# Read-out sums over four tokens with the products interleaved, and a second product buffer in the keys' place

## The chip, the cores and the metric

The kernel runs on one core of one Trainium2 chip. The metric is the device time of one execution in microseconds (us), lower is better. The engines are PE (TensorE; PEld is its weight load), DVE (VectorE), ACT (ScalarE), POOL (GpSimd) and SP, which only issues DMAs.

## What is computed

A vision tower: 32 images of 64 tokens with 256 features go through four layers, each with a mixer, a feed-forward part and layer norms. The change touches only the mixer of the second layer, a delta rule with 16 heads of 16 features (h = head, k, v = features):

```python
def step(S, inp):
    qt, kt, vt, at, bt = inp
    Sd = at[..., None, None] * S
    u = vt - jnp.einsum('bhk,bhkv->bhv', kt, Sd)
    Sn = Sd + bt[..., None, None] * kt[..., None] * u[:, :, None, :]
    o = jnp.einsum('bhk,bhkv->bhv', qt, Sn)
    return (Sn, o)
...
_, o = jax.lax.scan(step, S0, (tfirst(q), tfirst(k), tfirst(v), tfirst(a), tfirst(beta)))
o = o * jax.lax.rsqrt(jnp.mean(o * o, -1, keepdims=True) + EPS)
```

It is a recurrence over the 64 tokens. The read-out `o` of a token, the last line of the step, doesn't feed the next token.

## The kernel before

All data is fp32. In the delta layer (`delta_layer`) a partition holds one image and head for each of CG = 4 groups g, so that one state of a partition is 4 x 16 x 16 = 1024 numbers (g, v, k). It lies in two PSUM banks; the states of even and odd tokens have two banks each (`S[0]`, `S[1]`), and `halves` h = 0, 1 are the groups 0-1 and 2-3. Each engine runs its own program in order, and they meet at semaphores. One token t of the loop `for t in range(TOK)` is:

- DVE `read_keys(t)` (L1823, two halves of 512 elements): state times scaled key, PSUM to the tile `prod` (named made in the trace). It needs the state after token t-2; the effect of token t-1 is added as a column. Then DVE sums 18 numbers for each v (`tensor_reduce`, L1856) into `u`, which raises `u_made`.
- POOL makes the correction column of token t+1 (L1925), then the outer product `outer` of key and u (L1930, 1024 elements, tile xT_d in the trace).
- ACT places the values of a later token (L1603), writes the faded state of token t over the other pair of banks (`fade`, L1611, four instructions), and copies the fourth group's state to SBUF (`copy_last_group`, L1620), which raises `state_copied`.
- PE adds the outer product to the state in PSUM (`add_outer`, L1467): two matmuls of 512 columns with the identity as weights. An fp32 matmul shows as two records in the profile, so these are four records.
- Read-out of token j: DVE multiplies three groups of the state with the query (`read_queries(j)`, L1831, 768 elements, at its token j+3), POOL the fourth group (`read_copy(j)`, L1899, 256 elements, at its token j+2). The products go to the tile of the queries (chain_q), as `(r s n k)`: ring of two, two tokens s, 64 sums n = (g, v), and the 16 terms k next to each other. PE sums over k with the identity: `sum_pair(n, half)` (L1477) issues 8 matmuls of 128 columns (2 tokens x 64) behind `add_outer` of a token, 16 for a pair, so 16 records for each token. The moving operand takes one number in 16. ACT copies the 128 sums to the output tile (`store_pair`, L1624).
- Three times the squares of a stretch of outputs (CUTS) are made on ACT (`square_out`) and summed on PE (`sum_squares`, L1486), 32 records spread over six tokens.

PE's sums of token t stand between `add_outer(t)` and `add_outer(t+1)` in its queue. Pairs 0 to 30 (tokens 0 to 61) are read out that way; the last two tokens by DVE alone (`read_last`, L1839 and L1841). Behind the loop come the last squares, a Newton step and the norm of the outputs (L1871), which go out by DMA to the next stage.

The keys' tile (chain_k) is last read ahead of the loop, by `scale_keys` on DVE (L1796) and POOL (L1885).

Of the kernel before, what the change touches and what calls it, by code (L numbers as in the profile page):

```python
# [13 lines left out]
ALU = mybir.AluOpType  # L14
ACT = mybir.ActivationFunctionType
AX = mybir.AxisListType
# [10 lines left out]
TOK = 64  # L27
# [4 lines left out]
HD = D // HEADS  # L32
# [16 lines left out]
CG = 4  # L49
# [24 lines left out]
def bcast(ap, axis, n):  # L74

    ap = ap.unsqueeze(axis)
    shape = [int(s) for s in ap.shape]
    shape[axis] = n
    return ap.to_broadcast(shape)
# [1162 lines left out]


YS = 4
CUTS = (0, 18, 36, 52)
IN_STEPS = len(CUTS) - 1
TAIL = 2
LASTS = ((CUTS[-1], TOK - TAIL), (TOK - TAIL, TOK))
LAST = TOK - CUTS[-1]
ROW = HD + 2  # L1250
DIRECT = CG - 1
SUM_PARTS = ((0, 3), (3, 6), (6, 9), (9, 12), (12, 14), (14, HD))
# [29 lines left out]
def delta_layer(nc, sem, io, banks, H, ident, minus_half, token_rows, gate, chains, rates, front, chain, all_sent,  # L1282
# [15 lines left out]
    q, k, v, o = (chain[n] for n in "qkvo")  # L1298
    ka, kb, qt = (chain[n] for n in ("ka", "kb", "q_by_time"))
# [10 lines left out]
    prod = [prod_ring[:, i, :, :, :] for i in range(2)]  # L1310
    squares = w[:, :, :].rearrange("p c n -> p (c n)")[:, 0:HD * CG * CUTS[1]].rearrange("p (d n) -> p d n", d=HD)
    n_last = CG * HD * (TOK - TAIL - CUTS[-1])
    last_squares = [flat[:, n_prod + a:n_prod + b].rearrange("p (g d t) -> p g d t", g=CG, d=HD)
# [5 lines left out]
    Sc = [Sc_ring[:, i, :, :] for i in range(2)]  # L1319
    u_ring = rows_flat[:, n_zero + n_copy:n_zero + n_copy + 2 * CG * HD].rearrange("p (r g v) -> p r g v", r=2, g=CG)  # L1320
    u = [u_ring[:, i, :, :] for i in range(2)]
    products = q[:, :, :, :].rearrange("p g d t -> p (g d t)").rearrange("p (r s n k) -> p r s n k", r=2, s=2, k=HD)
    link = rate[:, :, 0, :]

    def state(b):
        return banks[:, b:b + 2, :].rearrange("p b (g v k) -> p (b g) v k", v=HD, k=HD)

    S = [state(0), state(2)]
    o_sum = [banks[:, b, 0:2 * CG * HD] for b in (5, 7)]
    halves = [slice(2 * h, 2 * h + 2) for h in range(2)]  # L1330
    summed_early, summed_late = slice(0, CUTS[-1]), slice(CUTS[-1], TOK)
    outs = [chains[n].rearrange("g (b h) (d t) -> g h d b t", h=HEADS, d=HD) for n in "qkv"]

    def o_n2(n):
        return banks[:, 6, CG * CUTS[n]:CG * CUTS[n + 1]].rearrange("p (g t) -> p g t", g=CG)

    def chunk_squares(n):
        return squares[:, :, 0:CG * (CUTS[n + 1] - CUTS[n])]
# [82 lines left out]
    def tensor(pe):  # L1421
# [41 lines left out]
        def add_outer(t, h):  # L1463
            if t:
                pe.wait_ge(sem(f"faded{h}"), t)
            pe.wait_ge(sem("outer_made"), t + 1)
            pe.matmul(S[t % 2][:, halves[h], :, :], ident[:, :], outer[t % 2][:, halves[h], :, :], start=False,  # L1467
                      stop=True, skip_group_check=True).then_inc(sem(f"state{h}"), 1)

        def sum_pair(n, half):  # L1470
            if half == 0:
                pe.wait_ge(sem("q_made"), 2 * n + 2)
                pe.wait_ge(sem("q_copy_made"), 2 * n + 2)
                if n > 1:
                    pe.wait_ge(sem("o_made"), n - 1)
            for k in range(HD // 2 * half, HD // 2 * (half + 1)):
                ins = pe.matmul(o_sum[n % 2].rearrange("p (s n) -> p s n", s=2), ident[:, :],  # L1477
                                products[:, n % 2, :, :, k], start=(k == 0), stop=(k == HD - 1))
            if half:
                ins.then_inc(sem("o_summed_pair"), 1)  # L1480

        def sum_squares(n, part):
            if part == 0:
                pe.wait_ge(sem("o_squared"), n + 1)
            for d in range(*SUM_PARTS[part]):
                ins = pe.matmul(o_n2(n), ident[:, :], chunk_squares(n)[:, d, :]  # L1486
                                .rearrange("p (g t) -> p g t", g=CG), start=(d == 0), stop=(d == HD - 1))
            if part == len(SUM_PARTS) - 1:
                ins.then_inc(sem("o_summed"), 1)
# [49 lines left out]
        for b in (1, 0):  # L1539
            for h in range(2):  # L1540
                ins = pe.matmul(banks[:, 2 * b + h, :], ident[:, :], zeros, start=True, stop=True)
                if b == 0:
                    ins.then_inc(sem(f"state{h}"), 1)
        for t in range(TOK):
            for h in range(2):
                add_outer(t, h)
            if t >= 3:
                sum_pair((t - 3) // 2, (t - 3) % 2)
            for n in range(IN_STEPS):
                if 0 <= t - CUTS[n + 1] - 5 < len(SUM_PARTS):  # L1550
                    sum_squares(n, t - CUTS[n + 1] - 5)
        sum_pair((TOK - TAIL) // 2 - 1, 1)

    def scalar(act):
        def norm(t):
# [46 lines left out]
        def place_values(t):  # L1602
            act.copy(prod[t % 2][:, :, :, HD + 1], v[:, :, :, t]).then_inc(sem("values_placed"), 1)  # L1603
# [12 lines left out]
        def copy_last_group(j):  # L1616
            act.wait_ge(sem("state1"), j + 2)
            if j >= 2:
                act.wait_ge(sem("q_copy_made"), j - 1)
            act.copy(Sc[j % 2], S[j % 2][:, DIRECT, :, :]).then_inc(sem("state_copied"), 1)  # L1620

        def store_pair(n):
            act.wait_ge(sem("o_summed_pair"), n + 1)
            act.copy(o[:, :, :, 2 * n:2 * n + 2], o_sum[n % 2].rearrange("p (s g d) -> p g d s", s=2, g=CG)  # L1624
                     ).then_inc(sem("o_made"), 1)

        def mean_out(n):
# [7 lines left out]
            act.activation(rn[:, :, at], rn[:, :, at], ACT.Exp, scale=-0.5).then_inc(sem("on_guess"), 1)  # L1635

        def square_out(n):
            act.wait_ge(sem("o_made"), CUTS[n + 1] // 2)
            if n:
                act.wait_ge(sem("o_summed"), n)  # L1640
            act.square(chunk_squares(n).rearrange("p d (g t) -> p g d t", g=CG),
                       o[:, :, :, CUTS[n]:CUTS[n + 1]]).then_inc(sem("o_squared"), 1)
# [69 lines left out]
        for t in range(TOK):  # L1712
            if t + 2 < TOK:
                act.wait_ge(sem("u_made"), t + 1)
                place_values(t + 2)
            if t:
                fade(t, 0)
                fade(t, 1)
            if 0 < t < TOK - 1:
                copy_last_group(t - 1)  # L1720
            if t >= 5 and t % 2:
                store_pair((t - 5) // 2)
            for n in range(IN_STEPS):
                if t == CUTS[n + 1] + 4:
                    square_out(n)
                if t == CUTS[n + 1] + 5 + len(SUM_PARTS):
                    mean_out(n)
        store_pair((TOK - TAIL) // 2 - 1)
        act.wait_ge(sem("on_mean"), IN_STEPS)
        guess(summed_early, 1)  # L1730
        act.wait_ge(sem("o_made"), (TOK - TAIL) // 2)
        square_last(0)
        act.wait_ge(sem("last_o"), 2)
        square_last(1)
# [4 lines left out]
    def vector(dve):  # L1739
        once = Tally(dve, sem("dve_once"))  # L1740
# [83 lines left out]
                                  bcast(ka[:, t, halves[h], :], 2, HD), ALU.mult).then_inc(sem(f"prod_made{h}"), 1)  # L1824

        def read_queries(j):
            n = j // 2
            dve.wait_ge(sem("state_copied"), j + 1)
            if n >= 2:
                dve.wait_ge(sem("o_summed_pair"), n - 1)  # L1830
            dve.tensor_tensor(products[:, n % 2, j % 2, 0:DIRECT * HD, :].rearrange("p (g v) k -> p g v k", g=DIRECT),  # L1831
                              S[j % 2][:, 0:DIRECT, :, :], bcast(qt[:, j, 0:DIRECT, :], 2, HD), ALU.mult
                              ).then_inc(sem("q_made"), 1)

        def read_last(j):
            for h in range(2):
                dve.wait_ge(sem(f"state{h}"), j + 2)
                dve.wait_ge(sem(f"faded{h}"), TOK - 1)
            once.mark(dve.tensor_tensor(prod[j % 2][:, :, :, 0:HD], S[j % 2], bcast(qt[:, j, :, :], 2, HD), ALU.mult))  # L1839
            once.settle()  # L1840
            dve.tensor_reduce(o[:, :, :, j], prod[j % 2][:, :, :, 0:HD], AX.X, ALU.add).then_inc(sem("last_o"), 1)  # L1841

        for t in range(TOK):
            if t == 3:
# [10 lines left out]
                dve.wait_ge(sem("outer_made"), t - 1)  # L1855
            dve.tensor_reduce(u[t % 2], prod[t % 2], AX.X, ALU.add).then_inc(sem("u_made"), 1)  # L1856
        read_queries(TOK - 3)
        dve.wait_ge(sem("u_made"), TOK)
        read_last(TOK - 2)
        read_last(TOK - 1)  # L1860
        for n, (a, b) in enumerate(LASTS):
            dve.wait_ge(sem("last_squared"), n + 1)
            once.mark(dve.tensor_reduce(n2[:, :, a:b], last_squares[n].rearrange("p g d t -> p g t d"), AX.X, ALU.add))
# [10 lines left out]
    def gpsimd(pool):  # L1874
# [17 lines left out]
            pool.tensor_tensor(dots, k[:, g, :, 1:], k[:, g, :, 0:TOK - 1], ALU.mult).then_inc(sem("neighbours"), 1)  # L1892

        def read_copy(j):
            n = j // 2
            pool.wait_ge(sem("state_copied"), j + 1)
            if n >= 2:
                pool.wait_ge(sem("o_summed_pair"), n - 1)
            pool.tensor_tensor(products[:, n % 2, j % 2, DIRECT * HD:CG * HD, :], Sc[j % 2],  # L1899
                               bcast(qt[:, j, DIRECT, :], 1, HD), ALU.mult).then_inc(sem("q_copy_made"), 1)  # L1900

        for t in range(T):
# [33 lines left out]
        x, y, z = (b[:, :, summed_early] for b in (n2, rn, tmp))  # L1936
# [1060 lines left out]
```

## Time and profile before

| | |
|---|---|
| median of 3 runs | 1424.85 us (1424.39 to 1436.09) |
| profiled execution: its own time | 1427.18 us |
| profiled execution: span from first to last instruction | 1425.2 us |
| mean granted TensorE clock | 0.953 of 2.4 GHz |
| busy in the span | PE 89%, DVE 55%, ACT 37%, POOL 33% |
| the delta layer's token loop | from 655.6 us, first DVE product, to 1009.5 us, start of the output norm |

The profile comes from one execution, so that durations and starts are of that one. Times in its views are from the start of the span. A group of the views is named by source line, engine and operation, then output and inputs; a busy time of overlapping instructions counts once.

### The profile page before, as it was taken

How to read it: one execution, taken by the hardware profiler on the slowest of the kernel's cores; microseconds unless marked ns; L12 is line 12 of the kernel's file. 1: busy time of each engine (PE TensorE's matmuls, PEld its weight loads, DVE VectorE, ACT ScalarE, POOL GpSimd, SP SyncE). 2: the span in 40 equal slices, each digit the busy share in tenths (PEclk: the TensorE clock that was granted, in tenths of full speed). 3: DMA queues.
4: the chain of work that ended last, by engine and by line, in shares of the span. 5: the costliest groups of instructions: out<-in, count | busy, mean ns of one | idle time of the engine just before them, and what ended most of it. 6: DMA issues, size and time to landing. Idle time of an engine off the chain costs nothing. (4 is left out here: it accounts for less than half of the span.)

```text
span 1425.2 us, 25953 instructions
## 1 busy us (share of the span) xinstructions
PE 1268.6 (89%) x9667; PEld 1022.5 (72%) x9667; DVE 788.2 (55%) x1721; ACT 531.5 (37%) x1318; POOL 464.6 (33%) x635
## 2 busy tenths in 40 slices
PE   7999994999999999873999999999589999978975
PEld 5666673888999999621777778777477777756753
DVE  4666666111121221798666666665467777642587
ACT  3554541121112121544444444343134444434456
POOL 0111111232333331544555455554122121101465
PEclk9999996999999999996999999999799999999985
DMA  4111102998888883790000000000200004006721
GB/s 144 31 46 46 35 13 74 354 369 316 323 316 335 316 324 133 194 267 2 1 1 1 0 1 0 1 1 1 78 12 11 11 9 182 2 1 253 220 73 60
DMA packets 82717, 162.31 MB, mean 114 GB/s; under 512 B 42977, under 2 KB 61537, under 8 KB 76577
## 3 DMA queue, kind: packets, MB, share of 16 engines
q1 hardware_dynamic: 63776, 114.44, 23.6%
q0 software_dynamic: 10224, 44.05, 8.0%
q10 hardware_dynamic: 8592, 2.16, 0.7%
q8 instruction: 78, 1.28, 0.4%
q14 instruction: 47, 0.38, 0.1%
HBM read 134.28 MB, written 26.35 MB: 113 GB/s over the span
## 5 line engine op out<-in xcount | busy, mean ns | idle before, releaser
L1477 PEld LDWEIGHTS banks<-chain_q,ident 128*128 128x128 f32 x992 | 202.8, 204 | 39.3 <-issue 24.2
L1477 PE MATMUL banks<-chain_q,ident 128*128 128x128 f32 x992 | 226.2, 394 | 0.0
L936 PE MATMUL banks<-rowsT,w_up 128*128 128x128 f32 x1716 | 201.2, 278 | 0.3 <-DMA w_up<-in_up_w 0.3
L936 PEld LDWEIGHTS banks<-rowsT,w_up 128*128 128x128 f32 x1716 | 198.0, 195 | 0.6 <-DMA w_up<-in_up_w 0.5
L1467 PE MATMUL banks<-xT_d,ident 128*128 128x512 f32 x256 | 124.4, 607 | 32.0 <-POOL xT_d L1930 28.1
L1611 ACT ACTIVATE banks<-banks,rate 128x256 f32<-128x256 f32 x252 | 100.6, 445 | 131.5 <-DVE made L1823 128.6
L1930 POOL TENSOR_TENSOR xT_d<-kb,ys 128x1024 f32<-128x1024 f32 x64 | 123.3, 1927 | 3.1 <-DVE ys L1856 3.0
L1823 DVE TENSOR_TENSOR made<-banks,ka 128x512 f32<-128x512 f32 x128 | 87.8, 690 | 58.2 <-PE banks L1467 52.7
L950 PE MATMUL banks<-w_down,hT 128*128 128x256 f32 x468 | 107.5, 379 | 0.6 <-DVE res L1115 0.6
L1105 DVE TENSOR_TENSOR hT<-banks,silu 64x128 f32<-64x128 f32 x39 | 11.0, 282 | 166.7 <-ACT silu L993 166.7
L1467 PEld LDWEIGHTS banks<-xT_d,ident 128*128 128x128 f32 x256 | 48.5, 197 | 68.7 <-issue 29.9
L950 PEld LDWEIGHTS banks<-w_down,hT 128*128 128x128 f32 x468 | 85.9, 190 | 11.0 <-issue 1.0
L1856 DVE TENSOR_REDUCE ys<-made 128x64 f32<-128x1152 f32 x64 | 86.6, 1353 | 5.7
L878 POOL DMA_DIRECT2D w_down<-in_down_w x39 | 22.2, 569 | 188.6 <-PE banks L950 180.4
L1831 DVE TENSOR_TENSOR chain_q<-banks,q_by_time 128x768 f32<-128x768 f32 x62 | 59.1, 953 | 41.2 <-PE banks L1477 41.2
L2090 POOL TENSOR_TENSOR agg_b<-agg_b,minus_half 128x1 f32<-128x1 f32 x48 | 28.4, 591 | 161.2 <-DVE agg_b L2316 160.0
L1925 POOL TENSOR_TENSOR made<-ys,rate 128x64 f32<-128x64 f32 x63 | 19.6, 311 | 155.5 <-DVE ys L1856 155.5
L983 ACT COPY rowsT<-banks 128x256 f32<-128x256 f32 x39 | 14.5, 373 | 145.6 <-PE banks L114 145.6
L468 PE MATMUL banks<-w_tok,patches 128*128 128x256 f32 x192 | 52.2, 411 | 6.7 <-DMA patches<-in_patches 6.7
L1115 DVE COPY res<-banks 128x256 f32<-128x256 f32 x39 | 16.6, 425 | 75.2 <-PE banks L950 75.2
L108 PE MATMUL banks<-ident 128*128 128x128 f32 x328 | 43.8, 291 | 12.1 <-PEq L92 12.1
L108 PEld LDWEIGHTS banks<-ident 128*128 128x128 f32 x328 | 41.9, 205 | 13.5 <-issue 13.0
(330 smaller groups left out, 2381.7 us busy)
## 6 DMA issues: line engine op xcount, KB each, us to landing
w_up<-in_up_w SPq DMA_DIRECT2D x39, 1408.0 KB, 5.9
w_down<-in_down_w POOLq DMA_DIRECT2D x39, 768.0 KB, 4.9
inter<-res_x SPq DMA_DIRECT2D x16, 512.0 KB, 2.8
back<-inter SPq DMA_DIRECT2D x15, 512.0 KB, 3.9
patches<-in_patches SPq DMA_DIRECT2D x16, 384.0 KB, 3.3
f<-in_f SPq DMA_DIRECT2D x6, 1024.0 KB, 11.7
ys<-token_rows SPq DMA_DIRECT2D x16, 256.0 KB, 2.9
xn_rows<-xn_all SPq DMA_DIRECT2D x16, 128.0 KB, 1.7
```

The costliest lines, as they stand in the source:

```text
L108: pe.matmul(out, ident, ident, start=True, stop=True, skip_group_check=True)
L468: ins = pe.matmul(X, patches[t % SLOTS_IN][:, c, :], w_tok[:, c, :], start=(c == 0), stop=(c == PC - 1), skip_group_check=True)
L936: ins = pe.matmul(out[:, m * P:(m + 1) * P], w[:, c, m * P:(m + 1) * P], x[:, c, :], start=(c == 0), stop=(c == 1))
L950: ins = pe.matmul(Y, hT[j % 2][:, c, :], w_down[j % DEEP][:, c, :], start=(c == 0), stop=(c == FULL))
L1467: pe.matmul(S[t % 2][:, halves[h], :, :], ident[:, :], outer[t % 2][:, halves[h], :, :], start=False, stop=True, skip_group_check=True).th ...
L1477: ins = pe.matmul(o_sum[n % 2].rearrange("p (s n) -> p s n", s=2), ident[:, :], products[:, n % 2, :, :, k], start=(k == 0), stop=(k == HD ...
L1611: ins = act.activation(S[t % 2][:, g, :, :].rearrange("p v k -> p (v k)"), S[(t + 1) % 2][:, g, :, :].rearrange("p v k -> p (v k)"), ACT.Copy,
L1823: dve.tensor_tensor(prod[t % 2][:, halves[h], :, 0:HD], S[t % 2][:, halves[h], :, :], bcast(ka[:, t, halves[h], :], 2, HD), ALU.mult).then ...
L1831: dve.tensor_tensor(products[:, n % 2, j % 2, 0:DIRECT * HD, :].rearrange("p (g v) k -> p g v k", g=DIRECT), S[j % 2][:, 0:DIRECT, :, :], ...
L1856: dve.tensor_reduce(u[t % 2], prod[t % 2], AX.X, ALU.add).then_inc(sem("u_made"), 1)
L1930: pool.tensor_tensor(outer[t % 2], bcast(kb[:, t, :, :], 2, HD), bcast(u[t % 2], 3, HD), ALU.mult).then_inc(sem("outer_made"), 1)
L2090: pool.tensor_tensor(agg[n][:, 1:2], agg[n][:, 1:2], minus_half[:, 0:1], ALU.pow).then_inc(sem(f"ln{n}_rstd"), 1)
```

## The change

- `sum_quad(m, part)` takes the place of `sum_pair`: four tokens (QUAD) are summed at once. A part is 4 matmuls of 256 columns, one part behind `add_outer` of each token from t = 5 on; so a token has 8 records of 256 columns in the place of 16 of 128.
- The products of four tokens are interleaved: `(n k s)`, so that the four tokens of one product stand next to each other and the terms k are four numbers apart. DVE and POOL write one number in four; PE reads runs of four numbers, 64 numbers apart.
- The ring of two buffers is now one in the queries' tile and one in the keys' tile (each whole).
- ACT's `store_quad` copies 256 sums for four tokens once, at every fourth token.
- TAIL is 4: quads 0 to 14 (tokens 0 to 59) are summed on PE. The products of tokens 60 and 61 are made as before, and summed by DVE (`sum_last(0, 2)`, 2048 terms); those of 62 and 63 are made by `read_last` into the same interleaved buffer and summed by `sum_last(2, 4)`.
- The first cut moves from 18 to 20, the squares' sums and means by a token, and the last `mean_out` behind the loop.

```diff
-CUTS = (0, 18, 36, 52)
+CUTS = (0, 20, 36, 52)
...
-TAIL = 2
+QUAD = 4
+TAIL = QUAD
+QUADS = (TOK - TAIL) // QUAD
...
-    products = q[:, :, :, :].rearrange("p g d t -> p (g d t)").rearrange("p (r s n k) -> p r s n k", r=2, s=2, k=HD)
+    products = [x[:, :, :, :].rearrange("p g d t -> p (g d t)").rearrange("p (n k s) -> p n k s", k=HD, s=QUAD)
+                for x in (q, k)]
...
     def state(b):
...
-    o_sum = [banks[:, b, 0:2 * CG * HD] for b in (5, 7)]
+    o_sum = [banks[:, b, 0:QUAD * CG * HD] for b in (5, 7)]
...
-        def sum_pair(n, half):
-            if half == 0:
-                pe.wait_ge(sem("q_made"), 2 * n + 2)
-                pe.wait_ge(sem("q_copy_made"), 2 * n + 2)
-                if n > 1:
-                    pe.wait_ge(sem("o_made"), n - 1)
-            for k in range(HD // 2 * half, HD // 2 * (half + 1)):
-                ins = pe.matmul(o_sum[n % 2].rearrange("p (s n) -> p s n", s=2), ident[:, :],
-                                products[:, n % 2, :, :, k], start=(k == 0), stop=(k == HD - 1))
-            if half:
-                ins.then_inc(sem("o_summed_pair"), 1)
+        def sum_quad(m, part):
+            if part == 0:
+                pe.wait_ge(sem("q_made"), QUAD * (m + 1))
+                pe.wait_ge(sem("q_copy_made"), QUAD * (m + 1))
+                if m > 1:
+                    pe.wait_ge(sem("o_made"), m - 1)
+            for k in range(HD // QUAD * part, HD // QUAD * (part + 1)):
+                ins = pe.matmul(o_sum[m % 2].rearrange("p (n s) -> p n s", s=QUAD), ident[:, :],
+                                products[m % 2][:, :, k, :], start=(k == 0), stop=(k == HD - 1))
+            if part == QUAD - 1:
+                ins.then_inc(sem("o_summed_quad"), 1)
         def sum_squares(n, part):
...
-            if t >= 3:
-                sum_pair((t - 3) // 2, (t - 3) % 2)
+            if t >= QUAD + 1:
+                sum_quad((t - QUAD - 1) // QUAD, (t - QUAD - 1) % QUAD)
...
-                if 0 <= t - CUTS[n + 1] - 5 < len(SUM_PARTS):
-                    sum_squares(n, t - CUTS[n + 1] - 5)
-        sum_pair((TOK - TAIL) // 2 - 1, 1)
+                if 0 <= t - CUTS[n + 1] - 6 < len(SUM_PARTS):
+                    sum_squares(n, t - CUTS[n + 1] - 6)
+        sum_quad(QUADS - 1, QUAD - 1)
     def scalar(act):
         def norm(t):
...
-        def store_pair(n):
-            act.wait_ge(sem("o_summed_pair"), n + 1)
-            act.copy(o[:, :, :, 2 * n:2 * n + 2], o_sum[n % 2].rearrange("p (s g d) -> p g d s", s=2, g=CG)
+        def store_quad(m):
+            act.wait_ge(sem("o_summed_quad"), m + 1)
+            act.copy(o[:, :, :, QUAD * m:QUAD * (m + 1)], o_sum[m % 2].rearrange("p (g d s) -> p g d s", s=QUAD, g=CG)
...
         def mean_out(n):
...
         def square_out(n):
-            act.wait_ge(sem("o_made"), CUTS[n + 1] // 2)
+            act.wait_ge(sem("o_made"), CUTS[n + 1] // QUAD)
...
-            if t >= 5 and t % 2:
-                store_pair((t - 5) // 2)
+            if t > 2 * QUAD and t % QUAD == 1:
+                store_quad((t - 2 * QUAD - 1) // QUAD)
...
-                if t == CUTS[n + 1] + 4:
+                if t == CUTS[n + 1] + 5:
...
-                if t == CUTS[n + 1] + 5 + len(SUM_PARTS):
+                if t == CUTS[n + 1] + 6 + len(SUM_PARTS):
...
-        store_pair((TOK - TAIL) // 2 - 1)
+        store_quad(QUADS - 1)
+        mean_out(IN_STEPS - 1)
...
-        act.wait_ge(sem("o_made"), (TOK - TAIL) // 2)
+        act.wait_ge(sem("o_made"), QUADS)
...
         def read_queries(j):
-            n = j // 2
+            m = j // QUAD
...
-            if n >= 2:
-                dve.wait_ge(sem("o_summed_pair"), n - 1)
-            dve.tensor_tensor(products[:, n % 2, j % 2, 0:DIRECT * HD, :].rearrange("p (g v) k -> p g v k", g=DIRECT),
+            if m >= 2:
+                dve.wait_ge(sem("o_summed_quad"), m - 1)
+            dve.tensor_tensor(products[m % 2][:, 0:DIRECT * HD, :, j % QUAD].rearrange("p (g v) k -> p g v k", g=DIRECT),
...
-            once.mark(dve.tensor_tensor(prod[j % 2][:, :, :, 0:HD], S[j % 2], bcast(qt[:, j, :, :], 2, HD), ALU.mult))
-            once.settle()
-            dve.tensor_reduce(o[:, :, :, j], prod[j % 2][:, :, :, 0:HD], AX.X, ALU.add).then_inc(sem("last_o"), 1)
+            once.mark(dve.tensor_tensor(products[QUADS % 2][:, :, :, j % QUAD].rearrange("p (g v) k -> p g v k", g=CG),
+                                        S[j % 2], bcast(qt[:, j, :, :], 2, HD), ALU.mult))
+        def sum_last(a, b):
+            dve.tensor_reduce(o[:, :, :, TOK - QUAD + a:TOK - QUAD + b].rearrange("p g d s -> p (g d) s"),
+                              products[QUADS % 2][:, :, :, a:b].rearrange("p n k s -> p n s k"), AX.X, ALU.add
+                              ).then_inc(sem("last_o"), 1)
...
-        dve.wait_ge(sem("u_made"), TOK)
+        dve.wait_ge(sem("q_made"), TOK - 2)
+        dve.wait_ge(sem("q_copy_made"), TOK - 2)
+        sum_last(0, 2)
...
+        once.settle()
+        sum_last(2, QUAD)
...
         def read_copy(j):
-            n = j // 2
+            m = j // QUAD
...
-            if n >= 2:
-                pool.wait_ge(sem("o_summed_pair"), n - 1)
-            pool.tensor_tensor(products[:, n % 2, j % 2, DIRECT * HD:CG * HD, :], Sc[j % 2],
+            if m >= 2:
+                pool.wait_ge(sem("o_summed_quad"), m - 1)
+            pool.tensor_tensor(products[m % 2][:, DIRECT * HD:CG * HD, :, j % QUAD], Sc[j % 2],
```

## Rows read from the trace of the kernel before

**Rows 1.** The page: busy time of each engine.

```profile
PE 1268.6 (89%) x9667; PEld 1022.5 (72%) x9667; DVE 788.2 (55%) x1721; ACT 531.5 (37%) x1318; POOL 464.6 (33%) x635
```

**Rows 2.** Stretches of the token loop: us, then busy us of each engine, granted clock.

```profile
660.75:672.60 11.85, 8.02 (x12) 2.44 (x12) 8.71 (x12) 5.55 (x16) 7.37 (x8) 0.84 0.00 0
680.00:780.00 100.00, 100.00 (x387) 78.15 (x386) 69.41 (x78) 45.82 (x129) 54.71 (x58) 1.00 0.00 1
```

**Rows 3.** Groups of the loop, 655 to 1010 us: busy us, mean ns | idle before.

```profile
L1477 PE MATMUL banks<-chain_q,ident 128*128 128x128 f32 x992 | 226.2, 394 | 0.0
...
L1856 DVE TENSOR_REDUCE ys<-made 128x64 f32<-128x1152 f32 x64 | 86.6, 1353 | 5.7
L1831 DVE TENSOR_TENSOR chain_q<-banks,q_by_time 128x768 f32<-128x768 f32 x62 | 59.1, 953 | 41.2 <-PE banks L1477 41.2
...
L1899 POOL TENSOR_TENSOR chain_q<-ys,q_by_time 128x256 f32<-128x256 f32 x62 | 45.2, 729 | 0.0
...
L1925 POOL TENSOR_TENSOR made<-ys,rate 128x64 f32<-128x64 f32 x63 | 19.6, 311 | 155.5 <-DVE ys L1856 155.5
...
L1486 PE MATMUL banks<-w_delta,ident 128*128 128x72 f32 x64 | 8.7, 268 | 0.0
```

**Rows 4.** Order of time, tokens 3 and 4, without sums: start, us.

```profile
668.85 1.35 DVE L1856 TENSOR_REDUCE ys<-made 128x64 f32<-128x1152 f32 x1
...
670.12 0.96 DVE L1831 TENSOR_TENSOR chain_q<-banks,q_by_time 128x768 f32<-128x768 f32 x1
...
670.54 1.93 POOL L1930 TENSOR_TENSOR xT_d<-kb,ys 128x1024 f32<-128x1024 f32 x1
671.00 1.28 DVE L1823 TENSOR_TENSOR made<-banks,ka 128x512 f32<-128x512 f32 x2
671.76 1.54 ACT L1611 ACTIVATE banks<-banks,rate 128x256 f32<-128x256 f32 x4 [1.21 <-DVE made L1823]
672.37 1.35 DVE L1856 TENSOR_REDUCE ys<-made 128x64 f32<-128x1152 f32 x1
...
672.63 1.98 PE L1467 MATMUL banks<-xT_d,ident 128*128 128x512 f32 x4 [1.53 <-ACT banks L1611]
673.21 0.40 ACT L1620 COPY ys<-banks 128x256 f32<-128x256 f32 x1
```

**Rows 5.** Order of time, one token in the middle.

```profile
816.65 0.42 PEld L1467 LDWEIGHTS banks<-xT_d,ident 128*128 128x128 f32 x2
...
818.60 3.65 PE L1477 MATMUL banks<-chain_q,ident 128*128 128x128 f32 x16
...
821.86 0.21 PEld L1467 LDWEIGHTS banks<-xT_d,ident 128*128 128x128 f32 x1
```

**Rows 6.** Order of time, matmuls of 256 columns in another stage.

```profile
303.31 2.76 PE L950 MATMUL banks<-w_down,hT 128*128 128x256 f32 x12
```

**Rows 7.** Groups around the loop: accesses with a step, and one held op.

```profile
L1788 DVE SCALAR_TENSOR_TENSOR f<-rn,rate 128x64 f32<-128x64 f32 x4 | 9.5, 2383 | 0.1
...
L1796 DVE TENSOR_TENSOR ka<-chain_k,f 128x1024 f32<-128x1024 f32 x4 | 7.7, 1922 | 0.1
...
L1871 DVE TENSOR_TENSOR chain_o<-chain_o,rn 128x1024 f32<-128x1024 f32 x4 | 4.6, 1221 | 0.0
...
L1863 DVE TENSOR_REDUCE n<-made 128x40 f32<-128x640 f32 x1 | 1.3, 1281 | 5.9 <-ACT made L1646 5.9
...
L1863 DVE TENSOR_REDUCE n<-made 128x8 f32<-128x128 f32 x1 | 0.3, 282 | 0.0
...
L1885 POOL TENSOR_TENSOR kb<-chain_k,f 128x1024 f32<-128x1024 f32 x4 | 9.4, 2360 | 13.0 <-DVE f L1784 13.0
```

**Rows 8.** Order of time, end of the loop.

```profile
987.24 1.35 DVE L1856 TENSOR_REDUCE ys<-made 128x64 f32<-128x1152 f32 x1
...
997.57 7.14 PE L1477 MATMUL banks<-chain_q,ident 128*128 128x128 f32 x32
...
1009.53 4.63 DVE L1871 TENSOR_TENSOR chain_o<-chain_o,rn 128x1024 f32<-128x1024 f32 x4
```


## Prediction

> **What bounds the kernel now.** I read the page first: PE is busy for 89% of the span, far ahead of the others [rows 1], but that is an average over four layers. The change touches only the token loop, so I cut out that stretch. Between 680 and 780 us PE is busy for 100.00 of 100 us at full granted clock, DVE for 69, POOL for 55 and ACT for 46 [rows 2]. PE is the bound there, and the groups of the loop say with what: 992 records of the read-out sums hold 226.2 us [rows 3].
>
> The order of time gives the token's sum. One token in the middle takes 821.86 - 816.65 = 5.21 us [rows 5]. Its 16 sum records take 3.65 us; the last has a tail of 0.39 (mean of one [rows 3]), so that they follow each other every (3.65 - 0.39)/15 = 0.217 us, 3.47 us a token. What is left for the four records of the outer product is 5.21 - 3.47 = 1.74 us. Squares come on top: 8.7 us / 64 = 0.136 us a record [rows 3], 96 records, 13 us in the whole loop.
>
> What else could be the bound is shown by the trace too. In tokens 3 and 4 the read-out products are already made, but no sums are queued yet: there DVE's reductions start at 668.85 and 672.37, 3.52 us apart [rows 4]. Between them DVE has no gap: reduction, query products (670.12), key products (671.00), next reduction. So 3.52 us is DVE's own token, 1.7 us below PE's. POOL needs 0.31 + 1.93 + 0.73, about 3.0 us [rows 3, 4]; ACT's fades and state copy are 1.54 + 0.40 [rows 4] and its copy of 64 values is small, about 2.3 us. Both fit.
>
> **PE's part of the change.** Removed: 16 records of 128 columns a token. Added: 8 records of 256. The trace doesn't show a moving operand in runs of four, so I bound it. From below: contiguous matmuls of 256 columns, 12 in 2.76 us with a tail of 0.38, are (2.76 - 0.38)/11 = 0.216 us each [rows 6]. From above: the columns cost what they cost now, 2 x 0.217 = 0.434 us. Today's 0.217 for 128 columns is as much as 256 contiguous ones take, so today's step of 64 bytes doubles the time of a column. The new operand has that kind of step once in four numbers. I take the lower end, 0.216, because three of four numbers are read as the contiguous rows' are; halfway cases are checked below. PE's token is then 1.74 + 8 x 0.216 = 3.47 us, and 3.47 + 0.82 = 4.29 us in the twelve tokens that also carry six records of squares.
>
> The Trainium skill (SBUF — State Buffer, the note on cachelines in its section on the DMA port swizzle) says that SBUF is read in lines of 16 bytes and that accesses to the same line run at full bandwidth, with two hits enough. By it the new reads, four numbers of one line, would cost the contiguous price, as in my sum; today's doubled column agrees with it.
>
> **DVE's part.** `read_queries` keeps its 768 elements and 953 ns [rows 3], but now writes one number in four. No row has a write with a step of 16 bytes. Lower end: nothing extra; a reduction over data with a step of 8 bytes takes 282 ns for 128 elements [rows 7], which is the same 155 ns + 1.04 ns an element that contiguous work has (1353 ns for 1152 [rows 3]). Upper end: a DVE product that writes with a step of 256 bytes takes 1922 ns for 1024 elements, its contiguous sister 1221 [rows 7]; a reduction that reads with a step of 40 bytes takes 1281 ns for 640 [rows 7]. Both are 155 ns + 1.73 to 1.76 ns an element. At that price the query products take 155 + 768 x 1.73 = 1480 ns, 0.53 us more. Between the ends I take the upper one: the row at 256 bytes is the only one of the same operation with the step on its output, and the penalty has its full size at 40 bytes already, so it looks like one that is paid or not, with nothing between. DVE's token becomes 3.52 + 0.53 = 4.05 us.
>
> **POOL and ACT.** `read_copy` writes with the same step. Its row is 729 ns [rows 3]; the POOL product with a strided output takes 2360 ns against 1927 without [rows 4, 7], 0.42 ns an element, so 256 elements cost 0.11 us at most. POOL's token is 3.1 us of 4.05: covered, also without the cover of DVE's price, as 3.1 is under 3.52. ACT's copy of 256 sums comes once in four tokens, about 0.4 us, and the first squares grow from 18 to 20 tokens; ACT has 2.3 us of work plus these in 4.05. In the three tokens where copy and squares (1.3 us) meet it is about 4.0 us: just covered, and a slip there costs some tenths.
>
> **Waits.** PE's part 0 of a quad waits for DVE's product of the fourth token and POOL's of the same token, and `add_outer` of the next token queues behind it. In the time of tokens 3 and 4, the matching product of DVE begins at 670.12 and would end at 671.60, POOL's begins when its outer product ends (672.47) and ends by 673.3; PE's four outer records run from 672.63 to about 674.35. So both are there before PE asks [rows 4]. In the other direction DVE and POOL wait for a free buffer at every fourth token, for sums that PE ends at about 672.63 + 3.47 = 676.1; DVE asks one token and more later (672.37 + 4.05 + 1.35 = 677.8). Nothing new stalls. PE's longer tokens with squares exceed 4.05 by 0.24 for four tokens in a row, about 1 us; the state's first half is summed by 672.63 + 0.87 = 673.5, and DVE takes it at 671.00 + 3.52 = 674.5 in the present rhythm [rows 4] and 0.5 us later in the new one, some 1.5 us of slack, so this is hidden.
>
> **The loop.** Before: from the reduction of token 3 at 668.85 to that of token 63 at 987.24 [rows 4, 8] are 318.4 us for 60 tokens. After: 60 x 4.05 = 243.0, and 0.5 for the products made before, 243.5 us. Gain 74.9 us.
>
> **The tail.** Before, from the last reduction's start to the output norm: 1009.53 - 987.24 = 22.3 us, held by PE, which is three tokens late and ends its sums at 997.57 + 7.14 = 1004.7 [rows 8]. After, PE's backlog is gone: outer product of token 63 about 3.4 us behind the reduction's start, end of the sums at about 8.7. DVE now has the longer chain. It can sum tokens 60 and 61 when POOL's last copy is made, at 1.35 + 0.1 + 1.93 + 0.84 = 4.2; that is 2048 terms with a step of 16 bytes, 155 + 2048 x 1.73 = 3.70, to 7.9; two products of 1024 at 1.93, to 11.8; the second sum 3.70, to 15.5. From the last output to the norm there were 1009.53 - 1004.7 = 4.8 us before [rows 8]; the early guess and most squares now lie beside DVE's sums, so I take 3.5, and come to 19.0. Gain 3.3 us. At contiguous prices the same chain is 4.2 + 2.28 + 2 x 1.22 + 2.28 + 3.3 = 14.5, a gain of 7.8.
>
> **Sum.** 74.9 + 3.3 = 78 us from the profiled execution's 1427.2 us gives 1349; the median of the runs is 2.3 below that execution, so 1346 us. The work behind the loop starts from its output and moves with it: the DMAs there are issued at the end of the loop.
>
> **Rivals.**
>
> *DVE's step is free.* For it: the reduction with a step of 8 bytes. Then DVE's token is 3.52 and PE's 3.47 plus squares. DVE gives 211 us for 60 tokens; of the 13 us of squares some 9 don't fit beside it: 220, a gain of 98, and the tail's 7.8: 106 us, 1319 us. Against it: only reads at 8 bytes support it. The same note of the Trainium skill says both that an access which changes the line pays and that a stride of 4 fp32 is free; by its first sentence the forecast holds, by its second this rival, at 1319 us.
>
> *PE gains nothing.* If 256 columns in runs of four still take 0.434, PE's token is 1.74 + 3.47 = 5.21 as before, and DVE's dearer products hide under it. Only the tail moves, by some 3 us of DVE that lie beside PE's backlog: 1420 to 1425 us. It decides from 0.29 a record on, where 1.74 + 8 x 0.29 passes 4.05; at 0.33, halfway, the token is 4.36 plus squares, 4.55 on average, and the time about 1378. For it: today's strided columns cost double, and every new run starts a new line. Against it: the share of such numbers falls from all to a quarter.
>
> *Slower: DVE held by POOL.* A DVE operation of 64 elements took 2383 ns where POOL's product of 2360 ran [rows 7]; at 155 ns + 1.04 ns an element it would be 222. If the query products with their spread output were held so behind POOL's outer product, which starts 0.4 us after them [rows 4], DVE's token would be 4.05 + 1.93 = 5.98: 359 us for 60 tokens, 40 more than before, and 1465 us. It decides from a token of 5.3 us, 1.8 us of added product time. Against it: the held operation has both inputs in SBUF; the query products have one in PSUM, as now, and aren't held today.
>
> **How the numbers follow.** The forecast has a chance of 0.56, the free step 0.22, a PE record in between (1360 to 1400 us) 0.08, PE without gain 0.11, the held DVE 0.03. The range takes in the forecast, the free step with a margin for its tail, and most of the middle: 1312 to 1385 us, about 0.85. Within 1% (1411 to 1439, what this measurement can't tell from no change) lies PE without gain. Faster by over 1%: 0.86; same 0.11; slower 0.03.
>
> **What the changed profile would show.** Right: 480 records of 256 columns, spaced 0.22 us; query products of about 1480 ns; reductions 4.05 us apart, with DVE busy nearly without gaps and PE idle 0.4 to 0.6 us a token; the wait of DVE's key products for PE gone. Products of 950 ns would show the free step, with PE and DVE both near full at 3.6 us a token. Records 0.43 us apart would show PE without gain, products of 3 us the held DVE. The forecast is wrong most easily in the price of one number in four on DVE.

## The result and the profile after

The changed kernel takes 1352.87 us in the median of 4 runs (1350.19 to 1357.56), beside 1427.19 us for the kernel before in 4 runs (1424.39 to 1436.09). The ratio is 0.9473 with a 95% interval of [0.9421, 0.9525]. By the medians that is 74 us less. The forecast was 1346 us with a range of 1312 to 1385. Times of the experiments below are medians too; one execution of terms_outermost, longer than its others at a lower granted clock (1360.49 us), is counted neither in its median nor in its ratio.

The page of the changed kernel, span and busy times, beside [rows 1]:

```profile
span 1352.3 us, 24890 instructions
...
PE 1173.6 (87%) x9155; PEld 908.6 (67%) x9155; DVE 818.0 (60%) x1721; ACT 526.1 (39%) x1302; POOL 466.7 (35%) x635
```

PE gave up 95 us of work and 512 records; DVE took on 30 us. As shares of the span, 89 to 87% and 55 to 60%, both look small, since the span covers four layers. The stretch view of the token loop shows more, beside [rows 2]:

```profile
680.00:780.00 100.00, 91.50 (x301) 55.44 (x301) 97.63 (x100) 54.31 (x152) 71.07 (x74) 0.98 0.00 1
780.00:910.00 130.00, 123.17 (x451) 78.77 (x450) 127.13 (x129) 72.96 (x205) 92.48 (x98) 1.00 0.00 1
```

DVE, the third busy time behind the length, went from 69% to 98%, PE from 100% to 92 and 95%. The bound has moved. The groups of the loop, the view of [rows 3], say what each operation costs now:

```profile
L1864 DVE TENSOR_REDUCE ys<-made 128x64 f32<-128x1152 f32 x64 | 86.6, 1353 | 5.7
L1827 DVE TENSOR_TENSOR made<-banks,ka 128x512 f32<-128x512 f32 x128 | 82.1, 681 | 3.2 <-PE banks L1470 3.2
L1480 PE MATMUL banks<-chain_q,ident 128*128 128x256 f32 x256 | 61.8, 385 | 0.0
L1480 PE MATMUL banks<-chain_k,ident 128*128 128x256 f32 x224 | 52.9, 379 | 0.0
L1835 DVE TENSOR_TENSOR chain_q<-banks,q_by_time 128x768 f32<-128x768 f32 x32 | 50.3, 1571 | 0.0
...
L1835 DVE TENSOR_TENSOR chain_k<-banks,q_by_time 128x768 f32<-128x768 f32 x30 | 47.1, 1569 | 0.2 <-ACT ys L1623 0.2
...
L1911 POOL TENSOR_TENSOR chain_q<-ys,q_by_time 128x256 f32<-128x256 f32 x32 | 23.5, 735 | 0.0
```

The sums are 480 records with 114.7 us of busy time, half of 226.2 [rows 3]. DVE's query products cost 1570 ns instead of 953. POOL's fourth group costs 735 instead of 729. The idle time of DVE ahead of its query products, 41.2 us before, is gone.

One token without squares, in order of time, beside [rows 5]:

```profile
796.89 1.35 DVE L1864 TENSOR_REDUCE ys<-made 128x64 f32<-128x1152 f32 x1
...
798.17 1.57 DVE L1835 TENSOR_TENSOR chain_q<-banks,q_by_time 128x768 f32<-128x768 f32 x1
...
798.98 1.89 PE L1480 MATMUL banks<-chain_k,ident 128*128 128x256 f32 x8
...
799.57 1.28 DVE L1827 TENSOR_TENSOR made<-banks,ka 128x512 f32<-128x512 f32 x2
...
800.34 1.54 ACT L1614 ACTIVATE banks<-banks,rate 128x256 f32<-128x256 f32 x4 [1.73 <-DVE made L1827]
...
800.94 1.35 DVE L1864 TENSOR_REDUCE ys<-made 128x64 f32<-128x1152 f32 x1
...
801.21 1.98 PE L1470 MATMUL banks<-xT_d,ident 128*128 128x512 f32 x4 [0.34 <-ACT banks L1614]
```

The reductions are 800.94 - 796.89 = 4.05 us apart and DVE goes from one operation to the next. The eight sum records follow each other every (1.89 - 0.38)/7 = 0.216 us. PE stands idle for 0.34 us ahead of the outer product and waits for ACT's fade, which waits for DVE's key products.

The end of the loop, beside [rows 8]:

```profile
914.39 1.35 DVE L1864 TENSOR_REDUCE ys<-made 128x64 f32<-128x1152 f32 x1
...
918.54 3.83 DVE L1847 TENSOR_REDUCE chain_o<-chain_k 128x128 f32<-128x2048 f32 x1 [1.31 <-POOL chain_k L1911]
...
922.28 3.83 DVE L1843 TENSOR_TENSOR chain_k<-banks,q_by_time 128x1024 f32<-128x1024 f32 x2
...
922.74 1.95 PE L1480 MATMUL banks<-chain_q,ident 128*128 128x256 f32 x8
924.72 0.37 ACT L1627 COPY chain_o<-banks 128x256 f32<-128x256 f32 x1 [5.83 <-PE banks L1480]
...
926.14 3.77 DVE L1847 TENSOR_REDUCE chain_o<-chain_k 128x128 f32<-128x2048 f32 x1
```

PE's sums end at 924.7, DVE's at 929.9: the tail is now DVE's. The output norm starts at 932.93. The two profiled executions can be cut at the same four events, the starts of the first key product, of the reductions of tokens 3 and 63, and of the norm:

| stretch (us) | before | after | difference |
|---|---|---|---|
| start to first key product | 655.6 | 656.8 | +1.2 |
| to the reduction of token 3 | 13.2 | 13.7 | +0.5 |
| 60 tokens | 318.4 | 243.9 | -74.5 |
| tail, to the output norm | 22.3 | 18.5 | -3.8 |
| norm to end | 415.7 | 419.4 | +3.7 |
| span | 1425.2 | 1352.3 | -72.9 |

### The profile page after: what moved, and what is told of

It reads as the page before. It is cut to its first block and busy times, and to the rows that moved or that the text cites. A ratio compares the mean times of both kernels' runs of the same rounds, so it can differ in the third digit from the quotient of the medians.

```text
span 1352.3 us, 24890 instructions
## 1 busy us (share of the span) xinstructions
PE 1173.6 (87%) x9155; PEld 908.6 (67%) x9155; DVE 818.0 (60%) x1721; ACT 526.1 (39%) x1302; POOL 466.7 (35%) x635
## 5 line engine op out<-in xcount | busy, mean ns | idle before, releaser
L1470 PE MATMUL banks<-xT_d,ident 128*128 128x512 f32 x256 | 130.8, 635 | 46.5 <-POOL xT_d L1942 26.1
L1614 ACT ACTIVATE banks<-banks,rate 128x256 f32<-128x256 f32 x252 | 97.4, 448 | 108.9 <-DVE made L1827 107.0
L1470 PEld LDWEIGHTS banks<-xT_d,ident 128*128 128x128 f32 x256 | 44.4, 193 | 101.3 <-ACT banks L1614 66.7
L1827 DVE TENSOR_TENSOR made<-banks,ka 128x512 f32<-128x512 f32 x128 | 82.1, 681 | 3.2 <-PE banks L1470 3.2
L983 ACT COPY rowsT<-banks 128x256 f32<-128x256 f32 x39 | 14.5, 373 | 146.2 <-PE banks L114 146.2
L1480 PEld LDWEIGHTS banks<-chain_q,ident 128*128 128x128 f32 x256 | 49.6, 194 | 20.4 <-issue 15.1
L1480 PE MATMUL banks<-chain_q,ident 128*128 128x256 f32 x256 | 61.8, 385 | 0.0
L108 PE MATMUL banks<-ident 128*128 128x128 f32 x328 | 41.6, 282 | 15.5 <-PEq L92 15.5
L1480 PEld LDWEIGHTS banks<-chain_k,ident 128*128 128x128 f32 x224 | 42.6, 190 | 17.7 <-issue 13.4
L1480 PE MATMUL banks<-chain_k,ident 128*128 128x256 f32 x224 | 52.9, 379 | 0.0
L108 PEld LDWEIGHTS banks<-ident 128*128 128x128 f32 x328 | 39.9, 197 | 16.9 <-issue 16.4
```

Of the source, the lines that this page charges most:

```text
L108: pe.matmul(out, ident, ident, start=True, stop=True, skip_group_check=True)
L1480: ins = pe.matmul(o_sum[m % 2].rearrange("p (n s) -> p n s", s=QUAD), ident[:, :], products[m % 2][:, :, k, :], start=(k == 0), stop=(k == ...
L1614: ins = act.activation(S[t % 2][:, g, :, :].rearrange("p v k -> p (v k)"), S[(t + 1) % 2][:, g, :, :].rearrange("p v k -> p (v k)"), ACT.Copy,
L1827: dve.tensor_tensor(prod[t % 2][:, halves[h], :, 0:HD], S[t % 2][:, halves[h], :, :], bcast(ka[:, t, halves[h], :], 2, HD), ALU.mult).then ...
```

## The experiments

Each kernel was timed beside the kernel before, and its ratio is to that. The theory was the prediction's: PE's price is that of its read pattern, DVE's that of its write pattern, and the loop goes at the pace of the slower of the two. The rivals were that the number of instructions matters, that a chain of waits through PE and ACT sets the token, and that steps or runs have other prices than I took.

**wide_only.** Quads and 256 columns stay, the interleaving goes:

```diff
-    products = [x[:, :, :, :].rearrange("p g d t -> p (g d t)").rearrange("p (n k s) -> p n k s", k=HD, s=QUAD)
+    products = [x[:, :, :, :].rearrange("p g d t -> p (g d t)").rearrange("p (s n k) -> p n k s", k=HD, s=QUAD)
```

The order of tokens and sums in the PSUM bank is turned with it, and so is ACT's copy from there.

> Quads, 256 columns and the second buffer as in the change, but the products of a token lie contiguous again, (s n k), so that PE reads one number in sixteen. Theory (what halves PE's time is the run of four, not the width of the matmul): a record costs 2 x 0.217 = 0.434 us, PE's token 1.74 + 8 x 0.434 = 5.21 us plus squares, the query product is back at 0.95 us, and the time is 1420 to 1428 us, within 0.5% of the kernel before. Rival (the gain comes from half as many instructions): records of about 0.22 to 0.3 us and 1320 to 1375 us.

Measured: 1423.12 us in the median of 10 runs, ratio 0.9963 [0.9935, 0.9991]. A token in its order of time:

```profile
756.45 1.90 PE L1470 MATMUL banks<-xT_d,ident 128*128 128x512 f32 x4
758.18 3.61 PE L1480 MATMUL banks<-chain_k,ident 128*128 128x256 f32 x8
761.62 1.90 PE L1470 MATMUL banks<-xT_d,ident 128*128 128x512 f32 x4
```

Eight records take as long as sixteen did: (3.61 - 0.61)/7 = 0.429 us each, and 761.62 - 756.45 = 5.17 us a token. Half the instructions at twice the columns, together with the second buffer and the new tail, are worth 0.4%. The rival falls.

**plain_writes.** The changed kernel, with DVE and POOL writing to a contiguous view of the same buffers, PE reading as in the change:

```diff
+    plain = [x[:, :, :, :].rearrange("p g d t -> p (g d t)").rearrange("p (s n k) -> p n k s", k=HD, s=QUAD)
+             for x in (q, k)]
...
-            dve.tensor_tensor(products[m % 2][:, 0:DIRECT * HD, :, j % QUAD].rearrange("p (g v) k -> p g v k", g=DIRECT),
+            dve.tensor_tensor(plain[m % 2][:, 0:DIRECT * HD, :, j % QUAD].rearrange("p (g v) k -> p g v k", g=DIRECT),
...
-            pool.tensor_tensor(products[m % 2][:, DIRECT * HD:CG * HD, :, j % QUAD], Sc[j % 2],
+            pool.tensor_tensor(plain[m % 2][:, DIRECT * HD:CG * HD, :, j % QUAD], Sc[j % 2],
```

> The changed kernel, but DVE and POOL write each token's products contiguously (another place of the same buffer), while PE reads runs of four as in the change; so the outputs of tokens 0 to 61 are sums of other products. Only the price of the writes is taken away. Theory (DVE's 1.57 us product is the bound of the loop): product 0.95 us, token 3.52 to 3.65 us, 25 to 32 us below the changed kernel: 1322 to 1330 us. Rival (the token is set by the chain through PE and ACT, and DVE only looks full): less than 8 us gained, 1345 to 1352 us.

Measured: 1323.0 us (4 runs), ratio 0.9256 [0.9211, 0.9302]. Its products, and two reductions in order of time:

```profile
L1837 DVE TENSOR_TENSOR chain_q<-banks,q_by_time 128x768 f32<-128x768 f32 x32 | 30.6, 955 | 0.0
...
L1837 DVE TENSOR_TENSOR chain_k<-banks,q_by_time 128x768 f32<-128x768 f32 x30 | 28.6, 954 | 0.2 <-ACT ys L1625 0.2
...
796.95 1.35 DVE L1866 TENSOR_REDUCE ys<-made 128x64 f32<-128x1152 f32 x1
...
800.46 1.35 DVE L1866 TENSOR_REDUCE ys<-made 128x64 f32<-128x1152 f32 x1
```

The products are back at 955 and 954 ns. A token without squares takes 800.46 - 796.95 = 3.51 us, DVE's own token of before; those with squares take 3.9 to 4.1, and the 60 tokens 217.8 us, 3.63 on average. So the write pattern costs the changed kernel 26 us in the loop. No chain of waits held the token at 4.06.

Both engines' writes were changed here. That the price is DVE's own, and not a disturbance by POOL's writes (whose operation changed by 7 to 9 ns), is seen in the tail of the changed kernel, where POOL is done when DVE makes the last two products:

```profile
L1843 DVE TENSOR_TENSOR chain_k<-banks,q_by_time 128x1024 f32<-128x1024 f32 x2 | 3.8, 2001 | 0.0
```

(2001 - 155)/1024 = 1.80 ns a number, against (1570 - 155)/768 = 1.84 in the loop. The tail kept its step in plain_writes and its length of 18.5 us.

**half_sums.** Half of PE's sums left out:

```diff
-            for k in range(HD // QUAD * part, HD // QUAD * (part + 1)):
+            for k in range(HD // QUAD * part, HD // QUAD * (part + 1), 2):
...
-                                products[m % 2][:, :, k, :], start=(k == 0), stop=(k == HD - 1))
+                                products[m % 2][:, :, k, :], start=(k == 0), stop=(k == HD - 2))
```

> The changed kernel with every second term k left out of the sums on PE (2 matmuls a part instead of 4), so the read-outs of tokens 0 to 59 hold half their terms. PE's token falls by 0.87 us. Theory (PE has slack now): the loop keeps its 4.06 us and the time stays within 3 us of the changed kernel, 1348 to 1355 us. Rival (PE's sums still delay the next outer product): up to 0.3 us a token, 1330 to 1342 us.

Measured: 1348.95 us (4 runs), ratio 0.945 [0.9409, 0.9491], not told apart from the change. In order of time:

```profile
794.96 1.03 PE L1480 MATMUL banks<-chain_q,ident 128*128 128x256 f32 x4
...
797.19 1.98 PE L1470 MATMUL banks<-xT_d,ident 128*128 128x512 f32 x4 [1.20 <-ACT banks L1614]
```

The sums of a token take 1.03 us instead of 1.89, and PE's idle time ahead of the outer product grows by the same 0.86, from 0.34 to 1.20. The 60 tokens take 243.76 us against 243.85. With plain_writes this settles the bound from both sides: taking work from PE gives nothing; taking 0.6 us from DVE's product gives 0.54 us in a token without squares and 0.43 on average, because PE's squares then show.

**pairs_in_quad.** Two tokens interleaved instead of four:

```diff
-    products = [x[:, :, :, :].rearrange("p g d t -> p (g d t)").rearrange("p (n k s) -> p n k s", k=HD, s=QUAD)
+    products = [x[:, :, :, :].rearrange("p g d t -> p (g d t)").rearrange("p (w n k s) -> p w n k s", w=2, k=HD, s=2)
...
-                                products[m % 2][:, :, k, :], start=(k == 0), stop=(k == HD - 1))
+                                products[m % 2][:, :, :, k, :], start=(k == 0), stop=(k == HD - 1))
```

The writes of DVE and POOL, the place of the sums in PSUM and the copies follow it.

> As the change, but two tokens interleaved instead of four, (w n k s) with w = 2 pairs and s = 2: DVE and POOL write one number in two (8 bytes apart), PE reads 256 columns in runs of two. Theory (DVE's price is that of steps over 8 bytes, and two numbers side by side are enough for PE): products 0.95 us, records 0.22 us, DVE's token 3.52 and PE's 3.47 plus squares, so about 3.65 us a token instead of 4.06: 60 x 0.41 = 25 us below the changed kernel, and some 4 more at the tail, 1322 to 1330 us. Rival A (any step costs DVE the same): 1.5 us products, time as the changed kernel, 1350. Rival B (runs of two save PE only half): records of 0.33 us, PE's token 4.4, and 1370 to 1380 us.

Measured: 1321.62 us (5 runs), ratio 0.9254 [0.9214, 0.9295]. In order of time:

```profile
784.33 1.35 DVE L1865 TENSOR_REDUCE ys<-made 128x64 f32<-128x1152 f32 x1
...
785.60 0.95 DVE L1836 TENSOR_TENSOR chain_q<-banks,q_by_time 128x768 f32<-128x768 f32 x1
...
786.47 1.28 DVE L1828 TENSOR_TENSOR made<-banks,ka 128x512 f32<-128x512 f32 x2
...
786.82 1.92 PE L1480 MATMUL banks<-chain_k,ident 128*128 128x256 f32 x8
...
787.84 1.35 DVE L1865 TENSOR_REDUCE ys<-made 128x64 f32<-128x1152 f32 x1
```

The token is 3.51 us, DVE's old floor. A write with a step of 8 bytes costs DVE nothing (0.95 us), and PE reads runs of two at the rate of contiguous numbers, (1.92 - 0.38)/7 = 0.220 us for 256. The 60 tokens take 218.3 us and the tail 16.4; the tail's gain of 2.1 us is half of the 4 expected. Both rivals of this run fall.

The two sentences of the Trainium skill's note on cachelines (SBUF — State Buffer, section on the DMA port swizzle), which spoke for different outcomes, can be weighed now. Two numbers in a 16-byte line were enough for both engines (DVE 0.95 us, PE 0.220 a record), as its first sentence says, and one in a line paid (1.57 and 0.429). "4 fp32" was not a free stride for DVE's writes. Steps between 8 and 16 bytes weren't tried.

**pair_runs_only.** The kernel before, with its pairs interleaved and nothing else: no quads, no second buffer, no other tail:

```diff
-    products = q[:, :, :, :].rearrange("p g d t -> p (g d t)").rearrange("p (r s n k) -> p r s n k", r=2, s=2, k=HD)
+    products = q[:, :, :, :].rearrange("p g d t -> p (g d t)").rearrange("p (r n k s) -> p r n k s", r=2, s=2, k=HD)
...
-                                products[:, n % 2, :, :, k], start=(k == 0), stop=(k == HD - 1))
+                                products[:, n % 2, :, k, :], start=(k == 0), stop=(k == HD - 1))
```

The writes, the order in PSUM and ACT's copy follow it.

> The kernel before with one edit: the two products of a pair interleaved, (r n k s) with s = 2, in the same ring in the queries' tile. Still 16 records of 128 columns a token, no second buffer, no quads. Theory (runs of two numbers are what PE needs, and steps of 8 bytes cost DVE nothing): a record falls from 0.217 us to 0.11 to 0.12, PE's token to 1.74 + 16 x 0.115 = 3.6 us plus squares, products stay at 0.95 us; loop 3.65 to 3.8 us a token, 1320 to 1335 us. Rival (128 columns are too short beside their weight load of 0.19 us): records stay near 0.19 us, PE's token 4.8 us plus squares, 1395 to 1405 us.

Measured: 1321.66 us (4 runs), ratio 0.9234 [0.9187, 0.928]. A token:

```profile
783.82 1.95 PE L1477 MATMUL banks<-chain_q,ident 128*128 128x128 f32 x16
...
784.82 1.35 DVE L1856 TENSOR_REDUCE ys<-made 128x64 f32<-128x1152 f32 x1
...
788.33 1.35 DVE L1856 TENSOR_REDUCE ys<-made 128x64 f32<-128x1152 f32 x1
```

The records follow each other every (1.95 - 0.27)/15 = 0.112 us instead of 0.217, and a token takes 3.51 us; the 60 tokens 220.3, against 218.3 with quads. So the width of the matmul and the second buffer bring 2 us in the loop between them, which the medians don't tell apart. The rival, that the weight load holds a short matmul, falls: each load is still 0.188 us long while the records follow each other every 0.112, so the loads overlap. This small edit is faster than both kernels. It leads the changed one by 31 us, of which the traces show 23.6 in the loop and 3.0 in the tail.

**terms_outermost.** The 16 terms outermost, so that PE reads 256 contiguous numbers and DVE writes with a step of 1024 bytes:

```diff
-    products = [x[:, :, :, :].rearrange("p g d t -> p (g d t)").rearrange("p (n k s) -> p n k s", k=HD, s=QUAD)
+    products = [x[:, :, :, :].rearrange("p g d t -> p (g d t)").rearrange("p (k n s) -> p n k s", k=HD, s=QUAD)
```

> The changed kernel with the products as (k n s): the 256 numbers of one term lie together, so PE reads 256 contiguous numbers, and DVE and POOL write with a step of 1024 bytes instead of 16. Theory (DVE's price is paid for any step over a line, whatever its size, and PE's run of four already has the full rate): products 1.57 us as with 16 bytes, records 0.216 us, time as the changed kernel within 3 us, 1347 to 1356 us. Rival (the price grows with the step, or several numbers in one place collide): products of 2 us or more, and 1375 us or more.

Measured: 1342.89 us (3 runs, 1339.22 to 1349.69), ratio 0.9403 [0.9333, 0.9472]. Its products:

```profile
L1835 DVE TENSOR_TENSOR chain_q<-banks,q_by_time 128x768 f32<-128x768 f32 x32 | 49.0, 1531 | 0.0
```

The products take 1531 ns, hardly less than with 16 bytes, and PE's records are no faster than with runs of four (61.3 us of busy time for 256, against 61.8). Of the steps measured here, 8 bytes cost DVE nothing, and from 16 to 1024 bytes the price doesn't grow. The median is 4 us below the 1347 to 1356 us that I gave, so that number was missed. The mechanism was not: 60 tokens take 241.7 us, 2.2 less than in the change, by the 0.04 us of the product. The rest of its lead of 10 us lies behind the loop (last section), where the change did nothing.

**changed_again.** The changed kernel, to see how much of the table above is its own.

> The changed kernel once more, for its spread and a second trace of the stages behind the loop, which took 419.4 us in its first trace against 415.7 us in that of the kernel before. Theory (that difference is of the execution, not of the change): median 1350 to 1354 us, loop 243.9 us again to 0.3 us, and stages behind the loop that take another time than 419.4. Rival (a later stage is slower by the change): 419 to 420 us there again.

Measured: 1353.3 us (4 runs), ratio 0.9462 [0.941, 0.9513]. The loop takes 244.2 us again, the tail 18.5, and the stages from norm to end 416.3 instead of 419.4, beside 415.7 in the kernel before. The rival, that the change slows a later stage, finds no support.

## Why the prediction was right

By its own steps:

- *PE's part.* Forecast 0.216 us a record, measured 0.216. PE's own token of 3.47 us can't be read in the changed kernel, where PE waits 0.34 us in a token without squares (0.4 to 0.6 were forecast). That the width brings nothing and the run all of it is shown by wide_only (0.429) and pair_runs_only.
- *DVE's part.* The choice between no price and 1480 ns was the one that decided between 1346 and 1319. No row lay between 8 and 40 bytes, so it was a judgement. Measured 1570 ns, the upper end and 90 ns over. The reason given, that the penalty doesn't grow with the step, holds from 16 to 1024 bytes (1570 and 1531 ns). That the token is 4.05 us to the hundredth is luck: the product is 0.62 us longer, not 0.53, but the next operation starts 1.40 us behind its start, where it was 0.88 before (671.00 - 670.12 [rows 4]). So two operations overlap by 0.09 us more than before, which nobody forecast and no run explains, and 0.52 is left.
- *The free step as rival.* Its price was about right: 1319 forecast, with 220 us in the loop, and plain_writes has 1323 with 217.8. That kernel frees the step in the loop alone; its tail is 18.5 us, not the 14.5 of this rival. The rival was wrong for the change, since a step of 8 bytes is free and one of 16 is not. The row at 8 bytes tells the price of a step of 8 bytes, for a write too, as pairs_in_quad shows, and says nothing of 16.
- *POOL.* Forecast up to 0.11 us more, measured 0.006. Steps of 16 and of 1024 bytes both left it at 735 and 734 ns. The comparison was of two different operations, and it isn't shown what made the one in [rows 7] longer. POOL lay beside DVE's token either way.
- *Waits.* No wait of PE for products shows up in the waits. From the reduction of token 3 on, DVE waits in the loop twice: 0.3 us for PE's outer product and 0.2 for ACT's state copy. In the whole loop its key products wait 3.2 us for PE, against 52.7 before. The longer tokens with squares are hidden: the reductions stay 4.05 us apart there, and half_sums shortens PE's work in all and gains nothing.
- *The loop.* 243.5 forecast, 243.9 measured; gain 74.9 against 74.5. Sixty tokens of 4.05 are 243.0. Of the rest, 0.8 lies in three early tokens. PE had waited up to 2.3 us ahead of an outer product there, its granted clock was 0.67 and 0.61 in two stretches of 4 us, and in the second its eight records took 3.11 us instead of 1.89. The forecast had 0.5 us there, for another reason.

```profile
684.00:688.00 4.00, 4.00 (x9) 2.40 (x8) 3.70 (x5) 2.01 (x7) 2.88 (x3) 0.61 0.00 0
...
685.87 3.11 PE L1480 MATMUL banks<-chain_q,ident 128*128 128x256 f32 x8
```

- *The tail.* 19.0 against 18.5, with DVE as its bound; the two sums over 2048 numbers take 3.8 us each and were forecast at 3.7. DVE's last sum ends 15.5 us behind the last reduction's start, as forecast.
- *The held DVE, PE without gain and the record in between.* No product of 3 us; records at the lower end. All three fell, with 3%, 11% and 8%.

The 7 us between 1346 and 1352.9 are not in the loop or its tail, where the difference is 78.3 us (74.5 + 3.8), and 78.2 were forecast. In the profiled execution 1.2 us lie ahead of the loop and 3.7 behind it. The rest is that of the medians: the forecast took off the 2.3 us by which the profiled execution lay above the kernel before's median of three runs, and with a fourth run that distance is gone (1427.18 and 1427.19); the changed kernel's is 1.1 us (1353.92 and 1352.87). The sum itself, 1349 less 2.3, is 1346.7 and was written down as 1346.

## What to carry to other kernels

When one engine is full, ask of its instructions what rate they run at before asking for fewer of them: 128 columns in the time of 256 pointed to the read pattern, and a new order of the data gave nearly all of the gain (wide_only has the rest of the change and 0.4%). Look for the smallest such change: a pair side by side was enough for the reader and free for the writer, while four side by side moved the price to the writer, which then became the bound. The edit that only pairs the numbers gained 106 us where the larger change gained 74. And where a trace has a few rounds without the work of the busy engine, as tokens 3 and 4 here, read the next bound from them.

## What was not expected

The stages behind the loop are untouched, but took from 409.8 to 424.5 us in the nine traces. Most of it arises 240 to 315 us behind the start of the output norm: in the shortest and the longest of these traces the same matmul starts at 237.3 and 241.3 us behind the norm, and a later one at 315.4 and 330.0. The stretch view shows the first 60 us of that. The column behind the busy times is the granted clock. The kernel before (415.7 us from norm to end):

```profile
1249.50:1309.50 60.00, 48.48 (x496) 37.25 (x498) 19.45 (x41) 22.54 (x53) 8.03 (x24) 0.91 0.30 113
```

The changed kernel (419.4 us):

```profile
1172.90:1232.90 60.00, 47.36 (x489) 36.09 (x491) 20.19 (x43) 20.86 (x48) 8.60 (x25) 0.89 0.27 99
```

terms_outermost (409.8 us):

```profile
1171.40:1231.40 60.00, 50.02 (x565) 38.15 (x566) 21.27 (x43) 25.55 (x60) 8.02 (x24) 1.00 0.38 139
```

pairs_in_quad (424.5 us):

```profile
1147.00:1207.00 60.00, 48.22 (x439) 37.19 (x438) 19.23 (x42) 18.19 (x41) 8.57 (x25) 0.77 0.22 78
```

There the engines wait for each other in short gaps, and PE is granted 1.00 of its clock throughout in one trace and spends part of the time at the lower of its two levels (1.2 instead of 2.4 GHz) in the others. The same eight records take 2.08 us at the lower level instead of 1.13, here first in pairs_in_quad and then in terms_outermost:

```profile
1152.10 2.08 PE L2168 MATMUL banks<-spread,H 64*128 64x256 f32 x8 [0.72 <-DVE probs_b L2360]
...
1172.62 1.13 PE L2167 MATMUL banks<-spread,H 64*128 64x256 f32 x8 [0.72 <-DVE probs_b L2359]
```

The traces with the highest and the lowest clock have the shortest and the longest rest, 15 us apart. That is of the size of the spread of a kernel's own runs (1317.74 to 1333.15 for pairs_in_quad), so it bounds what one trace of this kernel can tell. What decides which level is granted there was not tried.
